# FFN tail: the up products are taken out of PSUM by VectorE with both factors, in place of a ScalarE copy and a GpSimd product

## The chip, the cores and the metric

The kernel runs on one core of a Trainium2 chip. The metric is the device time of one execution in microseconds (us). The core has five engines with a queue each: TensorE (matmuls and transposes, results into PSUM), VectorE, ScalarE, GpSimd and SyncE, which issues the DMAs. They wait for each other by semaphores only; VectorE also waits for its own earlier results by an explicit drain.

## The reference

Two layers over x of 8 batches, 128 tokens and 512 features: a cross attention with 32 heads, an FFN with quantized operands, a channel attention with a small convolution, and a routed low-rank FFN, each with a layernorm ahead and a residual sum behind. The change touches only the quantized FFN:

```python
def fake_quant(t, axis):
    s = jnp.max(jnp.abs(t), axis=axis, keepdims=True) / QMAX
    s = jnp.maximum(s, 1e-08)
    q = jnp.clip(jnp.round(t / s), -QMAX - 1.0, QMAX) * s
    return t + jax.lax.stop_gradient(q - t)

def qlinear(x, w):
    xq = fake_quant(x, axis=-1)
    wq = fake_quant(w, axis=1)
    return jnp.einsum('bsh,oh->bso', xq, wq)
gate = qlinear(x, w_gate)
up = qlinear(x, w_up)
h = jax.nn.silu(gate) * up
return qlinear(h, w_down)
```

The inner width (INTER) is 1376.

## The kernel before, in words

A token tile is one batch: 128 tokens on the partitions, 512 features. Attention runs over 64 steps (32 heads for four batches, then 32 heads for the other four). The FFN of the first four batches is done inside the second half of these steps. The FFN of the last four, k = 0 to 3, is done after the attention, in a tail of its own from about 942 us to 1013 us. The tail's order is written out by hand, once for each engine; every engine takes its own queue in order.

For a tile k of the tail:

- VectorE (`token_steps`) finds the tile's maximum and quantizes it (L1471 to L1480); TensorE transposes it (`token_transposes`), ScalarE brings the transposed tile to SBUF as bf16 integers (`tokens_out`, L953).
- TensorE multiplies it with the gate weights into the PSUM tensor pA of three banks, in three chunks of 512, 512 and 352 columns, four matmuls each (`gate_products`, L2043). VectorE takes each chunk out in one instruction that multiplies by the step of the row (y_steps) and by the step of the weight's column (w_row[0]): `gate_rows`, L1489. ScalarE makes silu of the whole gate (`gated_silu`, L969).
- TensorE then writes the up products into the same three banks (`up_products`, L2043 again). A chunk waits until VectorE has taken the gate's chunk out of that bank. ScalarE copies each chunk out with the row's step (`up_out`, L961), and GpSimd, which works on SBUF only, multiplies the copy by the column's step (`up_rows` in its block, L684). The gate products of the next tile wait for ScalarE's copies to have left the banks (semaphore up_copy).
- VectorE (`hidden`) multiplies silu and up (L1496, 1376 columns), takes the maximum (L1498), makes step and reciprocal (L1500, L1502) and quantizes into h_mag (L1506). TensorE transposes h_mag in eleven pieces (`hidden_transposes`), ScalarE brings them to SBUF (`hidden_out`, L976 and L977), TensorE makes eleven down products into pD (`down_products`, L2078), VectorE takes them out with both factors (`down_rows`, L1514).
- The sum with the residual is GpSimd's for tiles 0 and 1 (`add_down`, L690) and VectorE's for 2 and 3 (`z_stats`, L1523). The statistics of the next layer follow: `z_stats` and `z_shift` on VectorE, the reciprocal root on GpSimd (`z_rstd`, L695), the normalized tile on ScalarE for tiles 0 and 1 (`z_normal`, L983), a transpose, and the split into two branches, for tiles 0 and 1 on GpSimd (`branches`, L700 and L702).

On GpSimd z_rstd(0) stands behind the up products of tile 3, and add_down(0) ahead of them. There are two buffers each for silu and up, and one for gate and for h_mag. ra is the matrix of the router and the low-rank factors; TensorE sums it over the features (L2106), ScalarE and GpSimd centre it (L1025, L710).

Of the kernel before, what the change touches and what calls it, by code (L numbers as in the profile page):

```python
# [13 lines left out]
F32 = mybir.dt.float32  # L14
# [4 lines left out]
ALU = mybir.AluOpType  # L19
# [3 lines left out]
P = 128  # L23
# [29 lines left out]
def layers_kernel(nc, x, cT, mask, bias, ln_w, wq, wk, wv, wo, w_gate, w_up, w_down,  # L53
# [3 lines left out]
    def sbuf(name, shape, dt=F32, stack=ctx):  # L57
        return stack.enter_context(nc.sbuf_tensor(name, shape, dt))
# [4 lines left out]
    def sem(name):  # L63
        return ctx.enter_context(nc.semaphore(name))

    with ctx:
# [165 lines left out]
        silu = [sbuf(f"silu{i}", [P, INTER], F32, inner_ffn) for i in range(2)]  # L232
        up = [e_up, sbuf("up1", [P, INTER], F32, inner_ffn)]
        h_mag = sbuf("h_mag", [P, INTER], F32, inner_ffn)
# [70 lines left out]
        s_d_added = sem("d_added")  # L305
        s_h_prod = sem("h_prod")
        s_o_last = sem("o_last")
# [63 lines left out]
        s_up = sem("up")  # L371
        s_up_copy = sem("up_copy")
        s_v = sem("v")
# [177 lines left out]
        def _(pool):  # L551
# [127 lines left out]

            def up_rows(k):  # L680

                for j, (c0, c1) in enumerate(chunks):
                    pool.wait_ge(s_up_copy, CHUNKS * k + j + 1)
                    g.tensor_tensor(up[k % 2][:, c0:c1], up[k % 2][:, c0:c1], w_row[1][:, c0:c1],  # L684
                                    ALU.mult).then_inc(s_up, 1)

            def add_down(k):
# [19 lines left out]
            token_rstd(1, HB)  # L707
            up_rows(0)
            pool.wait_ge(s_ra_mean, 1)
            g.tensor_tensor(ra[:], ra[:], ra_mean[:].to_broadcast([P, KT, E + ER]), ALU.subtract).then_inc(s_ra, 1)  # L710
            up_rows(1)
            up_rows(2)
            add_down(0)
            up_rows(3)
            z_rstd(0)
# [20 lines left out]
        def _(act):  # L736
# [217 lines left out]

            def up_out(k):

                if k >= 2:
                    act.wait_ge(s_h_prod, k - 1)
                for j, (c0, c1) in enumerate(chunks):
                    act.wait_ge(s_u_proj, CHUNKS * (HB + k) + j + 1)  # L960
                    a.activation(up[k % 2][:, c0:c1], pA[:, c0:c1], ACT.Copy,  # L961
                                 scale=y_steps[:, HB + k:HB + k + 1]).then_inc(s_up_copy, 1)

            def gated_silu(k):
# [52 lines left out]
            for k in range(1, HB):  # L1017
                tokens_normal(k)
            up_out(0)
            tokens_out(1)  # L1020
# [4 lines left out]
            a.activation(ra_mean[:, 0, :], ra_bank, ACT.Copy, scale=1.0 / D).then_inc(s_ra_mean, 1)  # L1025
            up_out(1)
            gated_silu(1)
            hidden_out(0)
            up_out(2)
            gated_silu(2)  # L1030
            hidden_out(1)
            up_out(3)
            gated_silu(3)
# [66 lines left out]
        def _(dve):  # L1100
# [382 lines left out]
            def gate_rows(k, j):  # L1483
# [3 lines left out]
                if j == 0 and later(k):  # L1487
                    dve.wait_ge(s_silu, HB + k)
                v.scalar_tensor_tensor(out=gate[:, c0:c1], in0=pA[:, c0:c1], scalar=y_steps[:, HB + k:HB + k + 1],  # L1489
                                       in1=w_row[0][:, c0:c1], op0=ALU.mult, op1=ALU.mult).then_inc(s_gate, 1)  # L1490

            def hidden(k):

                dve.wait_ge(s_silu, HB + k + 1)
                dve.wait_ge(s_up, CHUNKS * (k + 1))
                v.tensor_tensor(silu[k % 2][:], silu[k % 2][:], up[k % 2][:], ALU.mult).then_inc(s_h_prod, 1)  # L1496
                dve.drain()
# [81 lines left out]
            dve.wait_ge(s_y_normal, HB - 1)  # L1579
            token_steps(2, HB)  # L1580
            for j in range(CHUNKS):
                gate_rows(1, j)
            hidden(0)
            for j in range(CHUNKS):
                gate_rows(2, j)
            hidden(1)
            for j in range(CHUNKS):
                gate_rows(3, j)
            down_rows(0)
            hidden(2)  # L1590
            z_stats(0)
# [133 lines left out]
        def _(pe):  # L1725
# [321 lines left out]
            def gate_products(k):  # L2047
                pe.wait_ge(s_y_qT, k + 1)
                for j in range(CHUNKS):
                    if later(k):  # L2050
                        pe.wait_ge(s_up_copy, CHUNKS * (k - 1) + j + 1)
                    tail_inner(k, j, 0).then_inc(s_g_proj, 1)

            def up_products(k):
                for j in range(CHUNKS):
                    pe.wait_ge(s_gate, CHUNKS * (HB + k) + j + 1)
                    tail_inner(k, j, 1).then_inc(s_u_proj, 1)
# [40 lines left out]
            up_products(0)  # L2098
            token_transposes(1)
            gate_products(1)  # L2100
            token_transposes(2)
            token_transposes(3)
            pe.wait_ge(s_e_split, HB + 1)
            pe.wait_ge(s_const_in, 16 * 6)
            for kt in range(KT):
                last = mm(ra_bank, ones[:], ra[:, kt, :], start=kt == 0, stop=kt == KT - 1)  # L2106
            last.then_inc(s_ra_sum, 1)
            up_products(1)
            gate_products(2)
            hidden_transposes(0)  # L2110
            up_products(2)
            down_products(0)
            gate_products(3)
            hidden_transposes(1)
            up_products(3)
            down_products(1)
            hidden_transposes(2)
            down_products(2)
# [150 lines left out]
```

## Time and profile before

| what | value |
|---|---|
| median of three runs | 1065.99 us (1065.75 to 1067.38) |
| the profiled execution | 1069.71 us |
| its span, first to last instruction | 1068.0 us |
| mean granted TensorE clock | 0.973 |
| busy share of the span | TensorE 93%, VectorE 65%, ScalarE 48%, GpSimd 44% |
| chain of waits: shares of the span | TensorE 79%, VectorE 7%, GpSimd 3%, ScalarE 2% |

The profile is of one execution. A busy share is an average over stages that have different limits, so the table says little about the tail, which is some 7% of the span. There the timeline of each engine, the chain of waits in order of time and the busy time by stretch are to be read. The granted clock is that of TensorE as a share of full speed: 0.50 is 1.2 GHz and 1.00 is 2.4 GHz.

### The profile page before, as it was taken

What the parts mean: (1) busy time and instruction counts of PE and PEld (TensorE: products, weight loads), DVE (VectorE), ACT (ScalarE), POOL (GpSimd) and SP (SyncE); (2) the same over time, 40 slices, a digit from 0 to 9 for tenths busy, and PEclk for the clock granted to TensorE, in tenths of its full rate; (3) what the DMA queues carried; (4) which work ended last, traced back from release to release, by engine and by line L of the source; (5) the groups of instructions that cost most, each with busy time, mean ns of one, the idle gap of its engine ahead of it and who ended that gap; (6) DMA issues with size and microseconds to landing.
All of it is one profiled execution on the core that took longest, in us unless ns stands there. A gap on an engine that the chain in (4) does not pass through costs nothing.

```text
span 1068.0 us, 18238 instructions
## 1 busy us (share of the span) xinstructions
PE 996.8 (93%) x6004; PEld 843.0 (79%) x6004; DVE 697.6 (65%) x1827; ACT 512.6 (48%) x1328; POOL 467.5 (44%) x366
## 2 busy tenths in 40 slices
PE   5999999999999999999999999999999999869376
PEld 4888888888888888888888888888888888734263
DVE  5567565666577767677564575566567557678755
ACT  4454444444444445445543544445355354345561
POOL 4555444444444555443354344346435334226241
PEclk9999999999999999999999999999999999969768
DMA  6422222223333332333322222213222221000002
GB/s 219 161 92 87 95 95 89 91 95 96 96 97 98 98 97 83 104 112 98 106 84 84 85 67 72 83 42 98 73 74 84 80 69 53 23 21 1 0 2 79
DMA packets 50412, 87.71 MB, mean 82 GB/s; under 512 B 6368, under 2 KB 15200, under 8 KB 50336
## 3 DMA queue, kind: packets, MB, share of 16 engines
q1 hardware_dynamic: 50336, 86.76, 25.4%
q8 instruction: 40, 0.66, 0.2%
q14 instruction: 36, 0.29, 0.1%
HBM read 84.64 MB, written 2.10 MB: 81 GB/s over the span
## 4 chain that ended last, share of the span: by engine, by line
PE 79%; DVE 7%; issue 6%; POOL 3%; DVEq 2%; ACT 2%; DMA 1%; SPq 0%; POOLq 0%; ACTq 0%
PE pX L1731 15%; PE pX L1733 14%; PE pX L1732 14%; PE pT L1983 5%; PE oacc L1731 5%; PE oacc L1732 5%; PE oacc L1733 5%; PE pS L1915 5%; PE pS L1736 2%; PE pA L2043 1%; POOL wv_lo L570 1%; PE pX L1848 1%; PE pX L1904 1%; PE pT L1904 1%; PE pX L1736 1%
## 5 line engine op out<-in xcount | busy, mean ns | idle before, releaser
L570 POOL TENSOR_TENSOR wq_lo<-raw_q,wq_hi 128x512 fp32r<-128x512 f32 x64 | 82.6, 1290 | 264.2 <-DVE prob L1376 257.9
L1731 PE MATMUL pX<-wv_lo,cT_hi 128*128 128x256 f32 x512 | 149.5, 292 | 0.2 <-ACT q_sb L740 0.2
L1359 DVE TENSOR_TENSOR score<-pS,b_mask 128x512 f32<-128x512 f32 x64 | 44.2, 691 | 156.8 <-PE pS L1915 144.7
L868 ACT ACTIVATE prob<-score,neg_max 128x128 f32<-128x128 f32 x256 | 99.8, 391 | 97.4 <-DVE neg_max L1362 97.4
L1732 PE MATMUL pX<-wv_hi,cT_lo 128*128 128x256 f32 x512 | 144.3, 282 | 0.0
L1733 PE MATMUL pX<-wv_hi,cT_hi 128*128 128x256 f32 x512 | 144.2, 282 | 0.0
L570 POOL TENSOR_TENSOR wv_lo<-raw_v,wv_hi 128x1024 fp32r<-128x1024 f32 x32 | 77.1, 2409 | 121.9 <-ACT wv_hi L740 121.9
L740 ACT ACTIVATE v_sb<-pX 128x512 f32<-128x512 f32 x64 | 38.2, 597 | 163.6 <-PE pX L1733 163.6
L1731 PE MATMUL pX<-xT_lo,wq_hi 128*128 128x512 f32 x252 | 104.4, 414 | 5.7 <-POOL wq_lo L570 5.0
L1731 PE MATMUL oacc<-wo_lo,aT_hi 128*128 128x512 f32 x256 | 101.8, 398 | 3.5 <-DVE aT_lo L1351 2.3
L1731 PE MATMUL pX<-cT_lo,wk_hi 128*128 128x512 f32 x252 | 103.0, 409 | 0.0
L1732 PE MATMUL oacc<-wo_hi,aT_lo 128*128 128x512 f32 x256 | 101.0, 395 | 0.0
L1733 PE MATMUL oacc<-wo_hi,aT_hi 128*128 128x512 f32 x256 | 100.8, 394 | 0.0
L1733 PE MATMUL pX<-cT_hi,wk_hi 128*128 128x512 f32 x252 | 99.3, 394 | 0.0
L1732 PE MATMUL pX<-xT_hi,wq_lo 128*128 128x512 f32 x252 | 98.8, 392 | 0.0
L1732 PE MATMUL pX<-cT_hi,wk_lo 128*128 128x512 f32 x252 | 98.7, 392 | 0.0
L1733 PE MATMUL pX<-xT_hi,wq_hi 128*128 128x512 f32 x252 | 98.6, 391 | 0.0
L1732 PEld LDWEIGHTS pX<-wv_hi,cT_lo 128*128 128x128 f32 x512 | 98.0, 191 | 0.0
L1731 PEld LDWEIGHTS pX<-wv_lo,cT_hi 128*128 128x128 f32 x512 | 97.0, 190 | 0.5 <-ACT q_sb L740 0.5
L1733 PEld LDWEIGHTS pX<-wv_hi,cT_hi 128*128 128x128 f32 x512 | 97.0, 189 | 0.0
L740 ACT ACTIVATE wk_hi<-raw_k 128x512 fp32r<-128x512 f32 x64 | 40.4, 632 | 113.7 <-PE pX L1733 104.5
L570 POOL TENSOR_TENSOR wk_lo<-raw_k,wk_hi 128x512 fp32r<-128x512 f32 x64 | 83.0, 1298 | 26.7 <-ACT wk_hi L740 21.4
(308 smaller groups left out, 2377.4 us busy)
## 6 DMA issues: line engine op xcount, KB each, us to landing
raw_k<-in_wk SPq DMA_DIRECT2D x64, 256.0 KB, 2.8
raw_q<-in_wq SPq DMA_DIRECT2D x64, 256.0 KB, 3.5
raw_v<-in_wv SPq DMA_DIRECT2D x32, 512.0 KB, 3.9
raw_o<-in_wo SPq DMA_DIRECT2D x64, 256.0 KB, 2.6
b_raw<-in_bias SPq DMA_DIRECT2D x64, 64.0 KB, 2.5
g_raw<-in_w_gate SPq DMA_DIRECT2D x16, 172.0 KB
g_raw<-in_w_up SPq DMA_DIRECT2D x16, 172.0 KB
f_raw<-in_w_down SPq DMA_DIRECT2D x4, 688.0 KB, 4.1
```

Of the source, the lines that this page charges most:

```text
L570: g.tensor_tensor(w_lo[c][:], w_raw[c][:], w_hi[c][:].bitcast(F32), ALU.subtract).then_inc(s_w_lo[c], 1)
L740: return a.activation(dst, src, ACT.Copy)
L868: e = a.activation(prob[:, b, :], score[:, b, :], ACT.Exp, bias=neg_max[:, b:b + 1], accum_out=row_sum[:, b:b + 1])
L1359: v.tensor_tensor(score[:], pS[:].rearrange("p (b s) -> p b s", b=HB), b_mask[:], ALU.add).then_inc(s_scored, 1)
L1731: mm(dst, lh, rl, start=start, stop=False, skip_group_check=lint)
L1732: mm(dst, ll, rh, start=False, stop=False, skip_group_check=lint)
L1733: return mm(dst, lh, rh, start=False, stop=stop, skip_group_check=lint)
L1736: return mm(dst, src, ident, is_transpose=True, start=True, stop=True)
L1848: last = mm(pX0[:], e_hqT[0:deep, k * S:(k + 1) * S], wdT[0:deep, k, :], start=k == 0, stop=k == IT - 1)
L1904: last = mm(bank[:, 0:c1 - c0], y_qT[:, kt * S:(kt + 1) * S], w_rowT[up_half][:, kt, c0:c1], start=kt == 0, stop=kt == KT - 1)
L1915: last = mm(pS[:, cols], q_sb[:, cols], k_sb[:, cols], start=True, stop=True)
L1983: last = mm(pT[:, cols], v_sb[parity][:, b, heads], pT_sb[:, cols], start=True, stop=True)
```

## The change

The up products are taken out of PSUM by VectorE with both factors in one instruction, in a new `up_rows(k, j)` of VectorE's block, which is called three times at the head of `hidden(k)`. ScalarE's `up_out` and GpSimd's `up_rows` are gone, and with them the semaphores h_prod and up_copy and the second buffer of up. The gate products of the next tile wait for VectorE's `up_rows`. The orders by hand are changed with it: on VectorE hidden(k) stands ahead of gate_rows(k+1), and gate_rows(3) behind hidden(2); on TensorE the token transposes of tiles 1 to 3 and the sum of ra stand together ahead of gate_products(1), and each turn of a tile is gate, hidden transposes of the tile before, up, down of the tile before. A drain stands ahead of the product of silu and up. The hunks that only remove semaphores are left out here.

```diff
--- before.py
+++ after.py
@@ -230,7 +230,7 @@
         t_y = sbuf("t_y", [P, HB, D], F32, inner_ffn)
         t_yqT = [sbuf(f"t_yqT{k}", [P, KT * S], BF16, inner_ffn) for k in range(HB)]
         silu = [sbuf(f"silu{i}", [P, INTER], F32, inner_ffn) for i in range(2)]
-        up = [e_up, sbuf("up1", [P, INTER], F32, inner_ffn)]
+        up = e_up
         h_mag = sbuf("h_mag", [P, INTER], F32, inner_ffn)
         inner_ffn.close()
         coef = sbuf("coef", [P, B, KT, S], F32, post)
@@ -677,13 +675,6 @@
                 g.tensor_tensor(t_yrs[:, first:last], t_yve[:, first:last], neg_half[:, 0:last - first],
                                 ALU.pow).then_inc(s_y_rstd, 1)
 
-            def up_rows(k):
-
-                for j, (c0, c1) in enumerate(chunks):
-                    pool.wait_ge(s_up_copy, CHUNKS * k + j + 1)
-                    g.tensor_tensor(up[k % 2][:, c0:c1], up[k % 2][:, c0:c1], w_row[1][:, c0:c1],
-                                    ALU.mult).then_inc(s_up, 1)
-
             def add_down(k):
 
                 pool.wait_ge(s_d_used, HB + k + 1)
@@ -705,13 +696,9 @@
             token_rstd(0, 1)
             pool.wait_ge(s_y_var, 2)
             token_rstd(1, HB)
-            up_rows(0)
             pool.wait_ge(s_ra_mean, 1)
             g.tensor_tensor(ra[:], ra[:], ra_mean[:].to_broadcast([P, KT, E + ER]), ALU.subtract).then_inc(s_ra, 1)
-            up_rows(1)
-            up_rows(2)
             add_down(0)
-            up_rows(3)
             z_rstd(0)
             add_down(1)
             branches(0)
@@ -952,15 +939,6 @@
                 act.wait_ge(s_y_trans, k + 1)
                 a.activation(t_yqT[k][:], y_bank[k].bitcast(I16), ACT.Copy, bias=-OFFSET).then_inc(s_y_qT, 1)
 
-            def up_out(k):
-
-                if k >= 2:
-                    act.wait_ge(s_h_prod, k - 1)
-                for j, (c0, c1) in enumerate(chunks):
-                    act.wait_ge(s_u_proj, CHUNKS * (HB + k) + j + 1)
-                    a.activation(up[k % 2][:, c0:c1], pA[:, c0:c1], ACT.Copy,
-                                 scale=y_steps[:, HB + k:HB + k + 1]).then_inc(s_up_copy, 1)
-
             def gated_silu(k):
 
                 act.wait_ge(s_gate, CHUNKS * (HB + k + 1))
@@ -1016,20 +994,16 @@
             act.wait_ge(s_y_shift, 1)
             for k in range(1, HB):
                 tokens_normal(k)
-            up_out(0)
             tokens_out(1)
             gated_silu(0)
             tokens_out(2)
             tokens_out(3)
             act.wait_ge(s_ra_sum, 1)
             a.activation(ra_mean[:, 0, :], ra_bank, ACT.Copy, scale=1.0 / D).then_inc(s_ra_mean, 1)
-            up_out(1)
             gated_silu(1)
             hidden_out(0)
-            up_out(2)
             gated_silu(2)
             hidden_out(1)
-            up_out(3)
             gated_silu(3)
             hidden_out(2)
             z_normal(0)
@@ -1489,11 +1463,20 @@
                 v.scalar_tensor_tensor(out=gate[:, c0:c1], in0=pA[:, c0:c1], scalar=y_steps[:, HB + k:HB + k + 1],
                                        in1=w_row[0][:, c0:c1], op0=ALU.mult, op1=ALU.mult).then_inc(s_gate, 1)
 
+            def up_rows(k, j):
+
+                c0, c1 = chunks[j]
+                dve.wait_ge(s_u_proj, CHUNKS * (HB + k) + j + 1)
+                v.scalar_tensor_tensor(out=up[:, c0:c1], in0=pA[:, c0:c1], scalar=y_steps[:, HB + k:HB + k + 1],
+                                       in1=w_row[1][:, c0:c1], op0=ALU.mult, op1=ALU.mult).then_inc(s_up, 1)
+
             def hidden(k):
 
+                for j in range(CHUNKS):
+                    up_rows(k, j)
                 dve.wait_ge(s_silu, HB + k + 1)
-                dve.wait_ge(s_up, CHUNKS * (k + 1))
-                v.tensor_tensor(silu[k % 2][:], silu[k % 2][:], up[k % 2][:], ALU.mult).then_inc(s_h_prod, 1)
+                dve.drain()
+                v.tensor_tensor(silu[k % 2][:], silu[k % 2][:], up[:], ALU.mult)
                 dve.drain()
                 v.tensor_reduce(h_s[:, 0:1], silu[k % 2][:], AX.X, ALU.max, apply_absolute_value=True)
                 dve.drain()
@@ -1578,16 +1561,16 @@
             gate_rows(0, 2)
             dve.wait_ge(s_y_normal, HB - 1)
             token_steps(2, HB)
+            hidden(0)
             for j in range(CHUNKS):
                 gate_rows(1, j)
-            hidden(0)
+            hidden(1)
             for j in range(CHUNKS):
                 gate_rows(2, j)
-            hidden(1)
+            down_rows(0)
+            hidden(2)
             for j in range(CHUNKS):
                 gate_rows(3, j)
-            down_rows(0)
-            hidden(2)
             z_stats(0)
             down_rows(1)
             z_shift(0)
@@ -2048,7 +2031,7 @@
                 pe.wait_ge(s_y_qT, k + 1)
                 for j in range(CHUNKS):
                     if later(k):
-                        pe.wait_ge(s_up_copy, CHUNKS * (k - 1) + j + 1)
+                        pe.wait_ge(s_up, CHUNKS * (k - 1) + j + 1)
                     tail_inner(k, j, 0).then_inc(s_g_proj, 1)
 
             def up_products(k):
@@ -2096,25 +2079,24 @@
             pe.wait_ge(s_x1_done, 2)
             gate_products(0)
             up_products(0)
-            token_transposes(1)
-            gate_products(1)
-            token_transposes(2)
-            token_transposes(3)
+            for k in range(1, HB):
+                token_transposes(k)
             pe.wait_ge(s_e_split, HB + 1)
             pe.wait_ge(s_const_in, 16 * 6)
             for kt in range(KT):
                 last = mm(ra_bank, ones[:], ra[:, kt, :], start=kt == 0, stop=kt == KT - 1)
             last.then_inc(s_ra_sum, 1)
+            gate_products(1)
+            hidden_transposes(0)
             up_products(1)
+            down_products(0)
             gate_products(2)
-            hidden_transposes(0)
+            hidden_transposes(1)
             up_products(2)
-            down_products(0)
+            down_products(1)
             gate_products(3)
-            hidden_transposes(1)
+            hidden_transposes(2)
             up_products(3)
-            down_products(1)
-            hidden_transposes(2)
             down_products(2)
             z_transposes(0)
             hidden_transposes(3)
```

## Rows read from the trace of the kernel before

**Rows 1.** Chain of waits, whole span, from the page: shares by engine.
```profile
PE 79%; DVE 7%; issue 6%; POOL 3%; DVEq 2%; ACT 2%; DMA 1%; SPq 0%; POOLq 0%; ACTq 0%
```

**Rows 2.** Chain of waits in order of time: start us, us, what.
```profile
979.99 2.55 POOL xr L690
982.53 4.04 POOL up L684 x3
...
999.74 3.42 PE pD L2078 x11
```

**Rows 3.** Busy us (instructions) by stretch: PE, PEld, DVE, ACT, POOL; clock, DMA share, GB/s.
```profile
953.80:957.20 3.40, 1.50 (x7) 0.52 (x7) 2.88 (x7) 2.50 (x4) 0.82 (x1) 0.99 0.40 132
957.20:960.60 3.40, 2.74 (x12) 1.26 (x9) 3.08 (x5) 1.73 (x4) 1.90 (x3) 0.52 0.00 0
...
966.00:984.00 18.00, 17.88 (x107) 9.24 (x105) 16.54 (x22) 12.00 (x18) 13.82 (x10) 1.00 0.00 1
984.00:994.00 10.00, 3.90 (x28) 2.18 (x29) 8.77 (x12) 2.81 (x4) 6.73 (x6) 1.00 0.00 0
...
1023.00:1032.00 9.00, 7.82 (x33) 6.56 (x33) 4.05 (x10) 6.03 (x16) 4.82 (x5) 0.50 0.00 1
```

**Rows 4.** VectorE's timeline: start us, us, instruction, count, [idle before and what ended it].
```profile
955.65 0.49 DVE L1480 TENSOR_SCALAR t_y<-t_y,t_yinv 128x512 f32<-128x512 f32 x1
...
959.16 2.60 DVE L1480 TENSOR_SCALAR t_y<-t_y,t_yinv 128x512 f32<-128x512 f32 x2
962.58 0.75 DVE L1489 SCALAR_TENSOR_TENSOR e_gate<-pA,y_steps,g_row 128x512 f32<-128x512 f32 x1 [0.81 <-PE pA L2043]
...
965.44 1.58 DVE L1496 TENSOR_TENSOR silu<-silu,e_up 128x1376 f32<-128x1376 f32 x1
...
969.25 0.95 DVE L1506 TENSOR_SCALAR h_mag<-silu,h_s 128x1376 f32<-128x1376 f32 x1
970.53 1.90 DVE L1489 SCALAR_TENSOR_TENSOR e_gate<-pA,y_steps,g_row 128x512 f32<-128x512 f32 x3 [0.34 <-ACT silu L969]
972.35 1.58 DVE L1496 TENSOR_TENSOR silu<-silu,up 128x1376 f32<-128x1376 f32 x1
...
977.14 2.11 DVE L1489 SCALAR_TENSOR_TENSOR e_gate<-pA,y_steps,g_row 128x512 f32<-128x512 f32 x3
...
985.60 0.75 DVE L1514 SCALAR_TENSOR_TENSOR e_down<-pD,h_steps,sd_row 128x512 f32<-128x512 f32 x1
987.11 1.22 DVE L1534 SCALAR_TENSOR_TENSOR t_zshift<-t_zmv,t_zrs 128x1 f32<-128x1 f32 x1 [0.76 <-POOL t_zrs L695]
988.25 1.58 DVE L1496 TENSOR_TENSOR silu<-silu,up 128x1376 f32<-128x1376 f32 x1
...
992.05 1.77 DVE L1506 TENSOR_SCALAR h_mag<-silu,h_s 128x1376 f32<-128x1376 f32 x1
```

**Rows 5.** TensorE's timeline, the same columns.
```profile
956.86 2.66 PE L2043 MATMUL pA<-wuT,t_yqT 128*128 128x512 bf16 x8 [1.63 <-DVE e_gate L1489]
...
960.65 4.20 PE L2043 MATMUL pA<-wgT,t_yqT 128*128 128x512 bf16 x12 [0.71 <-ACT t_yqT L953]
...
965.13 1.15 PE L2106 MATMUL pD<-ra,ones 128*128 128x136 f32 x8
...
971.37 2.49 PE L2043 MATMUL pA<-wuT,t_yqT 128*128 128x512 bf16 x12
...
999.53 3.61 PE L2078 MATMUL pD<-wdT,e_hqT 128*128 128x512 bf16 x11
```

**Rows 6.** Timelines of the weight loads, ScalarE and GpSimd, the same columns.
```profile
961.48 0.15 PEld L2043 LDWEIGHTS pA<-wgT,t_yqT 128*128 128x128 bf16 x1 [0.28 <-issue]
...
960.48 1.35 ACT L969 ACTIVATE silu<-e_gate 128x1376 f32<-128x1376 f32 x1
...
968.18 4.04 POOL L684 TENSOR_TENSOR up<-up,u_row 128x512 f32<-128x512 f32 x3
...
991.83 1.26 POOL L702 TENSOR_TENSOR split<-zT,split 128x512 f32<-128x512 f32 x1
```

## The prediction: how the up products on VectorE move the tail

> **What bounds the kernel now.** I read the shares of the chain of waits first: TensorE holds most of it [rows 1], but nearly all of that lies in the attention part before 949 us, which the change does not touch. So I read the chain again, from 949 us on, in order of time. The FFN tail has three pieces there. From 960.65 to about 979 us the chain lies on TensorE. Then it goes through GpSimd: the sum of token tile 0 (2.55 us) and the three up products of tile 3 (4.04 us) [rows 2]. From 988.25 us it is VectorE's chain: product, maximum and quantization of tile 3, whose last instruction, h_mag(3), starts at 992.05 and ends at 993.82 [rows 4]. Everything behind, the statistics of tiles 1 and 2, the transpose of z(1), the eleven down products of tile 3 (3.42 us on the chain [rows 2]) and the convolution, hangs on that end and keeps its code. So the question is when h_mag(3) ends after the change.
>
> The table by stretch says what the change runs into: from 966 to 984 us TensorE is busy 17.88 of 18.00 us and VectorE 16.54, while GpSimd has 13.82 [rows 3]. VectorE is 92% full in the stretch in which it is to take up more.
>
> **What goes.** GpSimd loses twelve products, three of them 4.04 us [rows 6], ScalarE twelve copies out of PSUM. ScalarE is never the last arrival in this stretch but for short pieces, so its copies are worth nothing by themselves. SP's queue issues nothing here.
>
> **What VectorE gets.** Twelve instructions with both factors, PSUM in, SBUF out. Their row exists already: the gate's three chunks have this very form, 1.90 us busy for three, and 1.82 us from the first to the next instruction (970.53 to 972.35) [rows 4]. Behind them stands a new drain; between dependent instructions here that costs 0.09 us. So 1.91 us for a tile, 7.64 us for four. A tile then costs VectorE 1.82 (gate) + 1.91 (up) + 4.7 (965.44 to the end of h_mag(0) at 970.20, less the overlap with the next) = 8.4 us, against 6.5 before. TensorE's share of a tile is two times 2.3 for gate and up (12 matmuls, 2.49 us in the row, which overlaps its neighbours [rows 5]), 2.3 for the eleven down products at the same 0.21 each, and 0.6 for eleven transposes of 128 columns, 7.5 us. VectorE becomes the bound.
>
> **What VectorE gets back**, place by place, up to the end of h_mag(3) [rows 4]:
> - The two quantizing instructions before tile 1 take 2.60 us together beside GpSimd's products; one alone takes 0.49, so two back to back, less the overlap of 0.04 to 0.08 that neighbours show, about 0.94. Gain 1.66: they end at 960.1 in place of 961.76, and up(0) is ready at 959.5, so hidden(0) starts at once.
> - The wait of 0.81 before gate(1), and the gate's three chunks of tile 1, which take 2.86 (962.58 to 965.44) since TensorE feeds them late; now gate(1) is produced long before it is wanted. Gain 0.82 + 1.04.
> - The wait of 0.34 for silu before gate(2), and 2.11 against 1.90 for gate(3). Gain 0.5.
> - Between down_rows(1) at 985.60 and the product of tile 3 at 988.25 lie 2.65 us, of which work is 0.78 (down_rows 0.75, of which some overlaps, and about 0.1 for the 128x1 instruction); the rest is z_rstd(0) queued in GpSimd behind the up products, and a 128x1 instruction of 1.22 us beside GpSimd's sum. Gain 1.87.
> - h_mag(3), 1.77 us beside GpSimd's branch products against 0.95 for h_mag(0). Gain 0.83.
>
> Together 6.8 us.
>
> **New waits.** Hand schedule by these durations, 0.1 us for a signal. hidden(0) 960.1; its product 962.0, when silu(0) (960.48 + 1.35 [rows 6]) is done; h_mag(0) ends 966.75. gate_rows(1) 966.7 to 968.5. On TensorE the hidden transposes now stand before up(1) and cannot start before 966.85; up(1) follows 967.5 to 969.85, so up_rows(1) ends 0.2 late. On ScalarE hidden_out(0) is queued behind silu(1), which waits for gate_rows(1): it starts at 969.9 in place of right behind its transposes, down(0) starts at 971.4, gate(2), which is moved behind down(0), ends at 976.3. VectorE wants its last chunk at 976.7, so this is covered with 0.4 us to spare. up(2) costs 0.3, up(3) nothing, as statistics and down_rows(1) lie before it. Stalls 0.5 us. Moving the transposes of tokens 2 and 3 and the router's sum (1.15 us [rows 5]) ahead of gate(1) costs nothing: gate(1) then ends at 964.0 to 966.0 and is first wanted at 966.7. Sum: 7.64 - 6.8 + 0.5 = **+1.3 us**; h_mag(3) ends at 995.1.
>
> **The clock of that gap.** TensorE's granted clock was 0.99 (2.4 GHz) from 953.80 to 957.20, with 1.50 of 3.40 us busy and a gap of 1.63 at its end, and it then fell: 0.52 (1.2 GHz) in the next stretch [rows 3, 5]. From 966 on it stayed at 1.00 with no such gap. The change makes one: where TensorE went from gate(1) straight on, it now has nothing between the end of gate(1), 964.0 if the clock has risen by then, and the transposes at 966.85, a gap of 2.8 us. If the clock falls there, up(1) runs at 1.2 GHz. A matmul of 512 columns then starts every 0.43 us (0.15 of weight load and 0.28 of issue [rows 6]) and not every 0.21; chunk 0 takes 1.7 and chunk 1 1.7 against 0.86 each, and up_rows(1) ends 1.7 us later. This is on VectorE's chain. Bounds 0 and 1.7; I take 1.7, since the gap is longer than the one after which the clock fell. Later gaps (1.5 us at most by the schedule) do not exceed it, and from 984 to 994 us the clock stayed at 1.00 with 3.90 of 10 us busy [rows 3].
>
> **Two more bounds.** The down products of tile 3 took 3.61 us with part of them at the low clock [rows 5]; at 2.4 GHz eleven are 2.5, all at 1.2 GHz 4.7. So -1.1 to +1.1; I take 0, since the idle time before them keeps its shape. And h_mag(3) may still meet the branch products of tile 0 (1.26 us [rows 6]), for those shift with it: 0 if it starts first, +1.1 if behind. The schedule has it waiting when the first of the pair ends, so 0.
>
> That VectorE and GpSimd hold each other up is in the rows: 2.60 us against 0.94 while a GpSimd product ran, and GpSimd's sum took 2.55 [rows 2] against 1.26 for another 128x512 instruction of it [rows 6]. The Trainium skill, "SBUF — State Buffer", section "SBUF: two separate sides", says why: a shared port pair is held for a whole instruction, and the other engine blocks. By that rule the new instructions, with one SBUF tensor each, hold nobody up, and the sum is as above; the trace agrees (the three gate chunks at 970.53 ran beside GpSimd's products of tile 1, 968.18 to 972.22, and were not stretched [rows 4, 6]). The Trainium skill, "Perfetto Trace Analysis", section "Optimizing Scalar/DVE Operations", speaks against the change: with a saturated VectorE, work is better on ScalarE or even GpSimd. It adds that between VectorE and GpSimd this might not help. By the first sentence the time goes up, by the second it stays; the trace so far bears out the first.
>
> **Total.** The profiled execution took 1069.71 us, its span 1068.0, 1.71 around it; the median of the runs is 3.72 lower, and I apply the difference to it. +1.3 + 1.7 = +3.0: 1065.99 + 3.0 = **1069.0 us** (a profiled span near 1071).
>
> **Rivals.**
> - The clock holds through the gap, or has not risen yet when gate(1) starts, so that gate(1) itself, at half speed, fills it. For: gate(1) ran mostly at the low clock before, its row of 4.20 us [rows 5]. Against: TensorE is now busy without a pause up to it. Then +1.3 alone: 1067.3, within 0.2%. 22%.
> - Faster. One mechanism: the clock's level in the routed stage and in the last down products. From 1023 to 1032 us the clock was 0.50 with 7.82 us of TensorE busy [rows 3]; the same work at 2.4 GHz would give back at most 3.9, with the down products 5.0. A shift of the whole stage may let the rise fall earlier in the work. It must give back over 3.4 us to make the kernel faster by 0.2%; fully, 1065.99 + 1.3 - 5.0 = 1062.3. Against: nothing in the change fills the idle time before that stage. 10%.
> - The costly ends come together: the gap's clock, all down products at 1.2 GHz, h_mag(3) behind the branch products: 3.0 + 1.1 + 1.1 = +5.2, 1071.2; with the low clock in a second tile, 1072.9. 18%.
>
> **Chances.** Forecast 50% (1068.2 to 1070.4 by itself), rivals 22, 10 and 18. 0.2% is 2.1 us, about what a measurement of this kernel tells from no change. Slower 0.50 + 0.18 = 0.68, same 0.22, faster 0.10. The range leaves out the faster case and the top of the costly one: 1066.2 to 1071.8.
>
> **What would show it.** Right: in the profile after, VectorE has next to no idle time from 960 to 995 us; twelve up instructions near 0.63 us; the quantizing pair under 1 us; hidden products 8.4 to 8.7 us apart; TensorE with gaps; h_mag(3) ending 995 to 997; a clock near 0.5 somewhere between 967 and 971. Wrong: VectorE waiting for TensorE in each tile (then the low clock rules and I am too low), or h_mag(3) ending before 994 (then an up instruction costs less than the gate's, or more waits went than I count).

## The result, and the profile after

| | before | after |
|---|---|---|
| median of the plain runs | 1066.49 us (1065.75 to 1067.38) | 1073.06 us (1072.49 to 1073.42) |
| ratio | | 1.0059, 95% interval 1.0043 to 1.0075 |
| profiled execution, span | 1069.71, 1068.0 | 1073.42, 1071.7 |

The change makes the kernel slower by 6.3 us by the ratio (the medians differ by 6.6); 3.0 were forecast, with a range up to 1071.8 us. Between the two profiled spans lie only 3.7 us. That is the first sign that the profile of before was not an ordinary one.

VectorE's timeline of the kernel after, as in [rows 4]: start us, us, instruction, count, idle before and what ended it. L1470 is the new up instruction, L1479 the product of silu and up, L1463 the gate's.

```profile
953.11 0.16 DVE L1555 SCALAR_TENSOR_TENSOR t_yshift<-t_ymv,t_yrs 128x3 f32<-128x3 f32 x1 [0.90 <-POOL t_yrs L675]
...
958.97 0.88 DVE L1454 TENSOR_SCALAR t_y<-t_y,t_yinv 128x512 f32<-128x512 f32 x2
959.77 1.90 DVE L1470 SCALAR_TENSOR_TENSOR e_up<-pA,y_steps,u_row 128x512 f32<-128x512 f32 x3
961.76 2.71 DVE L1479 TENSOR_TENSOR silu<-silu,e_up 128x1376 f32<-128x1376 f32 x1
...
966.67 0.94 DVE L1489 TENSOR_SCALAR h_mag<-silu,h_s 128x1376 f32<-128x1376 f32 x1
967.52 1.89 DVE L1463 SCALAR_TENSOR_TENSOR e_gate<-pA,y_steps,g_row 128x512 f32<-128x512 f32 x3
970.77 0.75 DVE L1470 SCALAR_TENSOR_TENSOR e_up<-pA,y_steps,u_row 128x512 f32<-128x512 f32 x1 [1.35 <-PE pA L2026]
972.47 0.75 DVE L1470 SCALAR_TENSOR_TENSOR e_up<-pA,y_steps,u_row 128x512 f32<-128x512 f32 x1 [0.95 <-PE pA L2026]
973.65 0.58 DVE L1470 SCALAR_TENSOR_TENSOR e_up<-pA,y_steps,u_row 128x352 f32<-128x352 f32 x1 [0.42 <-PE pA L2026]
974.32 1.59 DVE L1479 TENSOR_TENSOR silu<-silu,e_up 128x1376 f32<-128x1376 f32 x1
...
983.42 1.59 DVE L1479 TENSOR_TENSOR silu<-silu,e_up 128x1376 f32<-128x1376 f32 x1
...
993.77 1.59 DVE L1479 TENSOR_TENSOR silu<-silu,e_up 128x1376 f32<-128x1376 f32 x1
...
997.57 0.94 DVE L1489 TENSOR_SCALAR h_mag<-silu,h_s 128x1376 f32<-128x1376 f32 x1
```

GpSimd's and TensorE's timelines of the same kernel, beside [rows 5]:

```profile
961.69 1.33 POOL L700 TENSOR_TENSOR ra<-ra,ra_mean 128x544 f32<-128x544 f32 x1 [8.61 <-ACT ra_mean L1002]
```
```profile
961.13 2.49 PE L2026 MATMUL pA<-wgT,t_yqT 128*128 128x512 bf16 x11
967.67 1.35 PE L1719 MATMUL pTb<-ident_b,h_mag 128*128 128x128 bf16 x11 [4.05 <-DVE h_mag L1489]
968.81 4.79 PE L2026 MATMUL pA<-wuT,t_yqT 128*128 128x512 bf16 x12
...
1004.21 4.33 PE L2061 MATMUL pD<-wdT,e_hqT 128*128 128x512 bf16 x11
```

And its busy time by stretch, the columns of [rows 3]:

```profile
962.00:966.00 4.00, 1.56 (x8) 0.68 (x7) 3.93 (x2) 0.00 (x0) 1.02 (x1) 1.00 0.00 0
966.00:974.00 8.00, 6.33 (x26) 3.23 (x27) 5.04 (x10) 2.63 (x3) 0.00 (x0) 0.57 0.01 2
974.00:984.00 10.00, 7.89 (x46) 3.87 (x46) 9.52 (x14) 2.64 (x3) 1.27 (x1) 1.00 0.00 0
```

From 974 to 984 us VectorE is busy 95% of the time and TensorE 79%; in [rows 3] it was 92 and 99%. The other two things to see are a first product that takes 2.71 us while its three sisters take 1.59, beside GpSimd's centring of ra (it starts 0.07 us ahead of the product), and the granted clock of 0.57 between 966 and 974 us, where VectorE waits three times for up(1), 2.7 us in all.

To compare executions that start the tail a little earlier or later, I count from one instruction that all have and that the change does not touch, the shift of the tokens (t_yshift; 953.11 us above). Each number is a time in VectorE's timeline less that (starts of the products of silu and up of tiles 0 and 2 and of down_rows(3), the end of h_mag(3)), and the span's end less that. The short names are those of the experiments; each line is one execution.

| execution | product 0 | product 2 | end of h_mag(3) | down_rows(3) | end of the span |
|---|---|---|---|---|---|
| before, on record | 12.13 | 26.51 | 40.51 | 49.86 | 114.69 |
| before_again | 10.66 | 25.02 | 39.03 | 49.02 | 111.94 |
| before_third | 9.76 | 23.79 | 37.79 | 47.05 | 111.70 |
| after | 8.65 | 30.31 | 45.40 | 55.47 | 118.59 |
| after_again | 8.65 | 28.11 | 44.30 | 54.95 | 118.81 |
| ra_late | 8.94 | 28.39 | 43.47 | 52.88 | 117.69 |
| fill16 | 8.65 | 27.62 | 42.71 | 52.81 | 115.91 |
| both12 | 8.84 | 26.70 | 41.79 | 52.08 | 115.36 |
| twice | 10.45 | 31.69 | 48.59 | 57.77 | 122.52 |
| zshift | 9.76 | 23.79 | 37.55 | 46.95 | 111.77 |
| gates_first | 9.59 | 23.63 | 37.63 | 46.95 | 111.69 |
| best1 | 10.18 | 24.92 | 38.68 | 48.60 | 111.51 |
| zshift2 | 9.76 | 23.80 | 35.49 | 46.06 | 109.04 |
| best2 | 9.59 | 23.61 | 35.31 | 45.99 | 109.09 |

### The profile page after: what moved, and what is told of

It is laid out like the page before. It is cut to its first block, busy times and chain, and to the rows that moved or that the text cites. A ratio compares the mean times of both kernels' runs of the same rounds, so it can differ in the third digit from the quotient of the medians.

```text
span 1071.7 us, 18208 instructions
## 1 busy us (share of the span) xinstructions
PE 995.3 (93%) x5988; PEld 841.7 (79%) x6004; DVE 702.3 (66%) x1839; ACT 505.6 (47%) x1316; POOL 451.1 (42%) x354
## 4 chain that ended last, share of the span: by engine, by line
PE 77%; DVE 9%; issue 6%; POOL 3%; ACT 2%; DVEq 2%; DMA 1%; SPq 0%; POOLq 0%; ACTq 0%
PE pX L1714 15%; PE pX L1716 14%; PE pX L1715 14%; PE pT L1966 5%; PE oacc L1714 5%; PE oacc L1715 5%; PE oacc L1716 5%; PE pS L1898 5%; PE pS L1719 2%; POOL wv_lo L568 1%; PE pT L1887 1%; PE pX L1831 1%; PE pX L1887 1%; PE pX L1719 1%; DMA raw_k<-in_wk 1%
```

## The experiments

### More profiles of the two kernels

No edit. The kernel before is profiled twice more, and the kernel after once more.

> The kernel before, unchanged, for a second profile. The profiled execution on record took 1069.71 us where its plain runs have a median of 1066.5; the changed kernel's took 1073.42 against 1073.1. Theory P (that one execution was late by where TensorE's clock rose and fell in the stages behind the FFN tail): the second profile has a span near 1065 and its tail ends h_mag(3) again near 993.8, with the difference behind 1003 us. Rival Q (a profile adds 3 us to this kernel): span near 1068 again.

> The kernel before once more. Counted from the shift of the tokens, the product of tile 2 started at 26.51 us in the profile on record, at 25.02 in before_again and at 23.79 in zshift, whose code is the same up to there. Theory B (the kernel before is bound by TensorE from up(0) to up(2), so its start moves with the clock that these products get, 4.20 or 2.50 us for gate(1)): this look lies between 23.7 and 26.6, and goes with the duration of up(0) and gate(1). Rival: the profile on record is the usual one, and this shows 26.5 again.

> The changed kernel once more. By theory B it is bound by VectorE and does not profit from an early high clock: its first product starts 8.6 to 9.0 us after the shift, takes 2.7 beside the centring of ra, and the end of h_mag(3) lies at 43 to 45.5, by how much of up(1) runs at the low clock. If the start varies as in the kernel before, by 2.7 us, theory B is wrong.

Measured: before_again 1067.48 us, span 1065.7; before_third 1067.49, span 1065.7; after_again 1074.45, span 1072.7. VectorE and TensorE in before_again, then the same in before_third:

```profile
962.60 1.90 DVE L1489 SCALAR_TENSOR_TENSOR e_gate<-pA,y_steps,g_row 128x512 f32<-128x512 f32 x3 [1.07 <-ACT silu L969]
...
991.02 1.77 DVE L1506 TENSOR_SCALAR h_mag<-silu,h_s 128x1376 f32<-128x1376 f32 x1
```
```profile
961.31 2.50 PE L2043 MATMUL pA<-wgT,t_yqT 128*128 128x512 bf16 x12 [0.71 <-ACT t_yqT L953]
```
```profile
990.02 1.77 DVE L1506 TENSOR_SCALAR h_mag<-silu,h_s 128x1376 f32<-128x1376 f32 x1
```
```profile
957.55 1.64 PE L2043 MATMUL pA<-wuT,t_yqT 128*128 128x512 bf16 x8 [1.37 <-DVE e_gate L1489]
...
960.31 2.50 PE L2043 MATMUL pA<-wgT,t_yqT 128*128 128x512 bf16 x12 [0.91 <-ACT t_yqT L953]
```

The same kernel ends h_mag(3) at 40.5, 39.0 or 37.8 us. The clock of up(0) and gate(1) goes with it: up(0)'s last eight matmuls took 2.66 us on record [rows 5], 2.86 in before_again and 1.64 in before_third, and gate(1) 4.20, 2.50 and 2.50. The execution on record was the slowest of the three, and its idle 0.81 us and stretched gate chunks of tile 1 [rows 4] were that clock. In before_again the three chunks take 1.90 us, behind a wait of 1.07 us for silu; in before_third VectorE does not wait for them at all. The quantizing pair ahead of them took 2.60, 1.90 and 2.17 us.

Theory B had the range right. That TensorE bounds this stretch is true of two executions of the three. In before_third the chain of waits leaves TensorE behind the router's sum and reaches the product of tile 1 over GpSimd:

```profile
964.64 1.90 POOL ra L710
966.53 4.00 POOL up L684 x3
970.63 1.59 DVE silu L1496
```

Rival Q is out, since the spans are 1065.7 us. Part of Theory P fell: it had h_mag(3) end where it did, and the difference behind. About half of the difference of the spans to before_again, 1.5 us of 2.75 counted from the shift, lies ahead of h_mag(3).

The start of the kernel after does not take part in this: its first product starts at 8.65 us in both profiles, though up(0) had the high clock in the first (1.63 us) and mostly the low one in the second (2.70 us). Two things differ behind it. VectorE, then GpSimd in after_again:

```profile
962.54 1.59 DVE L1479 TENSOR_TENSOR silu<-silu,e_up 128x1376 f32<-128x1376 f32 x1
...
996.15 2.04 DVE L1489 TENSOR_SCALAR h_mag<-silu,h_s 128x1376 f32<-128x1376 f32 x1
```
```profile
963.66 1.66 POOL L700 TENSOR_TENSOR ra<-ra,ra_mean 128x544 f32<-128x544 f32 x1 [9.81 <-ACT ra_mean L1002]
...
996.20 1.26 POOL L693 TENSOR_TENSOR split<-zT,split 128x512 f32<-128x512 f32 x1
```

My expectation for the product missed: 2.71 us in one execution and 1.59 in the other. The router's sum stands behind up(0), so with the low clock the centring comes later, here 1.12 us after the product has started, and the product is not stretched. And h_mag(3) takes 2.04 us beside a branch product of tile 0, in place of 0.94: 1.1 us of the 44.30 are that.

### Holding back the centring of ra

```diff
             pool.wait_ge(s_ra_mean, 1)
+            pool.wait_ge(s_gate, CHUNKS * (HB + 2) + 1)
             g.tensor_tensor(ra[:], ...
```

> The changed kernel, with GpSimd's centring of ra held back until VectorE has taken the first gate chunk of tile 2. Theory L (the first product of silu and up took 2.71 us in place of 1.58 since it met that centring on the shared port): it takes 1.6, h_mag(0) ends 1.1 us earlier and the time falls by 1.1, to about 1072.0. Rival C (only TensorE's clock in the gap before up(1) matters, VectorE waits there anyway): the product is shorter, the wait for up(1) longer by as much, and the time stays at 1073.

Measured: 1072.41 us, ratio to before 1.0052 (1.0035 to 1.0069), 0.7 us under the kernel after and not to be told from it by the intervals. The rows say more:

```profile
962.35 1.59 DVE L1480 TENSOR_TENSOR silu<-silu,e_up 128x1376 f32<-128x1376 f32 x1 [0.39 <-ACT silu L948]
...
970.11 0.75 DVE L1471 SCALAR_TENSOR_TENSOR e_up<-pA,y_steps,u_row 128x512 f32<-128x512 f32 x1 [1.22 <-PE pA L2027]
971.36 1.24 DVE L1471 SCALAR_TENSOR_TENSOR e_up<-pA,y_steps,u_row 128x512 f32<-128x512 f32 x2 [0.50 <-PE pA L2027]
```

The product takes 1.59 us with the centring out of its way (it ran at 978.23), as Theory L had it, but this run does not show the cause. In this profile up(0) had the low clock (2.99 us), and in after_again, with the low clock and no edit, the product takes 1.59 us as well. What speaks for Theory L is the set of the profiles: 2.71 us in both executions in which the centring starts just ahead of the product (after, and fill16 below, 961.27 against 961.34), 1.59 in every other one of the changed kernel. No run holds the centring back in an execution in which the two would have met. Rival C is not borne out: the waits for up(1) are 1.7 us, not longer than the 2.7 of the kernel after, and they are 1.7 in after_again too (0.78 and 0.96).

### Filling TensorE's gap

```diff
             gate_products(1)
+            for i in range(16):
+                mm(pZ[:], ident_b[:], w_rowT[0][:, i % KT, 0:512], start=True, stop=True)
             hidden_transposes(0)
```

> The changed kernel with 16 matmuls of 128x512 into an unused bank between gate_products(1) and hidden_transposes(0), 3.45 us of work at 2.4 GHz in a gap of 4.05 us; their result is used by nothing. Theory C (the gap lets the clock fall, and up(1) at 1.2 GHz makes VectorE wait 2.7 us): granted clock 1.00 from 962 to 990 us, the waits of 1.35, 0.95 and 0.42 us before the up chunks of tile 1 fall to under 0.3 in all, time 2.9 us less, about 1070.2. Rival W (VectorE waits for up(1) because the transposes stand ahead of it, whatever the clock): waits of over 1 us stay, time within 1 us of 1073.

Measured: 1071.34 us, ratio 1.0046 (1.0030 to 1.0063). VectorE, then the busy time by stretch:

```profile
968.98 2.10 DVE L1470 SCALAR_TENSOR_TENSOR e_up<-pA,y_steps,u_row 128x512 f32<-128x512 f32 x3
```
```profile
966.00:974.00 8.00, 6.08 (x37) 2.92 (x36) 7.63 (x10) 2.64 (x3) 0.00 (x0) 1.00 0.00 0
```

The clock stays at 1.00, up(1)'s three chunks take 2.10 us with their waits in place of 3.46 and 1.35 ahead of them, and h_mag(3) ends at 42.71 in place of 45.40, 2.7 earlier where 2.9 were expected. Theory C holds, and W falls: 0.2 us of waits are left. This pair, after and fill16, has the high clock at up(0) and the stretched first product in both. The other pair, ra_late and both12 below, has the low clock at up(0) and no stretched first product; there the filled gap is worth 43.47 - 41.79 = 1.7 us. The gap ahead of the hidden transposes was 4.05 us in the first case and 2.90 in the second. The plain runs of after and fill16 differ by 1.7 us, the lower of the two; how often each kind of execution comes, no run tells.

### Both together

The two edits above, with 12 matmuls.

> Both of these together, with 12 matmuls in place of 16 since the gap is 1.1 us shorter. If the two costs are separate and additive: 1073.1 - 1.1 - 2.9 = 1069.1, h_mag(3) ends at about 994.5 us, which would leave the 1.3 us of the sum for VectorE's added work alone against 993.6. If one hides behind the other: no faster than the better of the two.

Measured: 1071.46 us, ratio 1.0037 (1.0022 to 1.0051). h_mag(3) ends at 41.79 us: 3.6 before the kernel after, where the two expected effects add to 4.0. 41.79 is to the digit what the prediction's sum has without a clock term (995.1 less 953.31). So VectorE's side of the sum was right as a whole, and still the kernel is 0.37% slower than before, 3.9 us and not the 1.3 of the sum. What was wrong is the other side of the comparison: 40.51 as the kernel before's end. Against the other two profiles 41.79 is +2.8 and +4.0.

The expected 1069.1 us missed for a reason of the same kind. It takes two effects, read in one execution of the kernel after in which both were full, off the median of the plain runs; in after_again one of the two was not there and the gap was 2.62 us. By the plain runs it is the other expectation that came: 1071.46 is no faster than fill16's 1071.34.

### The up instructions twice

```diff
                 dve.wait_ge(s_u_proj, CHUNKS * (HB + k) + j + 1)
+                v.scalar_tensor_tensor(out=up_more[:, c0:c1], in0=pA[:, c0:c1], ...)
                 v.scalar_tensor_tensor(out=up[:, c0:c1], in0=pA[:, c0:c1], ...
```

> The kernel of both12 with each of VectorE's twelve up instructions issued twice, the first time into a buffer that nothing reads. Theory V (VectorE is the bound of the tail, so its added work stands on the path in full): 4 x 1.8 = 7.3 us more on VectorE, less the 0.5 us of waits that it covers; the end of h_mag(3), counted from the shift of the tokens (t_yshift), goes from 41.8 to 48.6 us and the time rises by 6.8, to about 1078. Rival T (TensorE or the chain over the transposes is the bound, and the up instructions lie half beside it): under 4 us more.

Measured: 1077.97 us, ratio 1.0102 (1.0087 to 1.0118), 6.5 us over both12. VectorE at tile 3, from the shift at 953.98:

```profile
994.04 0.74 DVE L1472 SCALAR_TENSOR_TENSOR up_more<-pA,y_steps,u_row 128x512 f32<-128x512 f32 x1
994.70 0.74 DVE L1474 SCALAR_TENSOR_TENSOR e_up<-pA,y_steps,u_row 128x512 f32<-128x512 f32 x1
...
1001.63 0.94 DVE L1493 TENSOR_SCALAR h_mag<-silu,h_s 128x1376 f32<-128x1376 f32 x1
```

h_mag(3) ends at 48.59, 6.80 later, as Theory V had it. Work on VectorE stands on the path in full in the changed tail, but for the waits that it covers; Rival T, with under 4 us, is out.

### Taking GpSimd out of VectorE's way in the kernel before

If GpSimd's chain cost the kernel before 1.9 us at tile 3, moving one small step should bring them back without more work for VectorE. The edits are to the kernel before; in zshift the step stands ahead of the drain, in zshift2 (the second diff) behind the maximum.

```diff
                 v.tensor_tensor(silu[k % 2][:], ...).then_inc(s_h_prod, 1)
+                if k == HB - 1:
+                    z_shift(0)
                 dve.drain()
...
             down_rows(1)
-            z_shift(0)
             hidden(3)
```

> The kernel before with one small step moved: z_shift(0) stands between the product and the maximum of tile 3, not ahead of the product, so VectorE does not wait there for GpSimd's up products and root. Theory G (GpSimd's chain cost the kernel before 1.9 us at this place, as the prediction's sum has it): the product of tile 3 starts 1.6 us earlier (it still waits for the last up product), h_mag(3) ends 37.4 us after the shift of the tokens in place of 39.0, time 1.6 us less, 1065.3. Rival H (the place is covered, what hangs on z_shift(0) is then late): within 0.5 us of the kernel before.

Measured: ratio 1.0000 (0.9991 to 1.0009). VectorE and GpSimd:

```profile
983.69 1.59 DVE L1496 TENSOR_TENSOR silu<-silu,up 128x1376 f32<-128x1376 f32 x1 [0.33 <-POOL up L684]
985.20 1.23 DVE L1536 SCALAR_TENSOR_TENSOR t_zshift<-t_zmv,t_zrs 128x1 f32<-128x1 f32 x1
...
988.65 1.93 DVE L1508 TENSOR_SCALAR h_mag<-silu,h_s 128x1376 f32<-128x1376 f32 x1
```
```profile
984.06 2.35 POOL L690 TENSOR_TENSOR xr<-xr,e_down 128x512 f32<-128x512 f32 x1
```

From product 2 to product 3 it is now 6.87 us in place of 8.44: the 1.57 are there. From product 3 to the end of h_mag(3) it is 6.89 in place of 5.57: GpSimd's sum takes 2.35 us in place of 1.26, beside the product; z_shift(0), a 128x1 instruction, takes 1.23 beside the sum, and h_mag(3) 1.93 beside the branch products. Neither theory had this: the gain is real, and 1.3 us of it are given back before h_mag(3) ends, where VectorE and GpSimd meet again.

```diff
                 v.tensor_reduce(h_s[:, 0:1], silu[k % 2][:], ...)
+                if k == HB - 1:
+                    z_shift(0)
```

> The kernel before with z_shift(0) behind the maximum of tile 3. In the run zshift, with it ahead of the maximum, the product of tile 3 came 1.57 us earlier, but 1.3 us were given back: z_shift(0) took 1.23 us beside GpSimd's sum and h_mag(3) 1.93 beside the branch products. Theory S (all of it is the shared port, so a step later both are clear of it): z_shift(0) takes 0.15, h_mag(3) 0.95 and ends before the branch products begin; from the product of tile 2 to the end of h_mag(3) 11.8 us in place of 14.0, time 2.2 less, about 1064.7. Rival D (what follows h_mag(3) does not wait for it, or GpSimd's steps collide elsewhere): within 0.7 us of the kernel before.

Measured: 1065.05 us against 1066.55, ratio 0.9986 (0.9976 to 0.9995).

```profile
983.91 1.59 DVE L1496 TENSOR_TENSOR silu<-silu,up 128x1376 f32<-128x1376 f32 x1 [0.33 <-POOL up L684]
985.60 1.59 DVE L1498 TENSOR_REDUCE h_s<-silu 128x1 f32<-128x1376 f32 x1
987.10 0.15 DVE L1536 SCALAR_TENSOR_TENSOR t_zshift<-t_zmv,t_zrs 128x1 f32<-128x1 f32 x1
987.81 0.94 DVE L1508 TENSOR_SCALAR h_mag<-silu,h_s 128x1376 f32<-128x1376 f32 x1
```

z_shift(0) is 0.15, h_mag(3) 0.94, and from product 2 to the end of h_mag(3) it is 11.7 us (14.0 before), as Theory S expected; of 2.3 us in the tail the plain runs show 1.5. GpSimd's sum had ended at 986.63, so z_shift(0) at the end of the maximum no longer met it.

### Gate chunks of tile 0 first

```diff
-            gate_rows(0, 0)
+            for j in range(CHUNKS):
+                gate_rows(0, j)
             dve.wait_ge(s_y_normal, 1)
             token_steps(1, 2)
-            gate_rows(0, 1)
-            gate_rows(0, 2)
```

> The kernel before with VectorE taking out all three gate chunks of tile 0 before it quantizes tile 1. Up(0) on TensorE then follows gate(0) without its gap of 1.6 us. Theory E (from 957 to 984 us the kernel before is bound by TensorE, so an earlier start counts): gate(1) starts 1.2 us earlier and h_mag(3) with it, time 1.2 less, 1065.7. Rival: quantizing tile 1 becomes late by the 1.2 us of the two chunks, gate(1) starts when it did, and the time stays.

> The kernel before with both of these. If both count and add: 1.6 + 1.2 = 2.8 us less than the kernel before, 1064.1. If the first start is not on the path, the 1.6 alone.

> The same with all gate chunks of tile 0 taken out before tile 1 is quantized, which alone measured nothing (ratio 1.0001). If that stays so: the time of zshift2. If the earlier start shows once GpSimd is out of the way: up to 1.2 us less, 1063.5.

Measured: alone 1.0001 (0.9992 to 1.0010), no gain, so Theory E is not borne out. Counted from the shift, gate(1) starts at 5.76 us, 0.55 earlier than in before_third and not 1.2, and product 0 at 9.59 against 9.76. As in before_third the chain then goes over GpSimd's centring (2.29 us here) and its three up products (4.01), which took 1.90 and 4.00 there. With zshift (best1) 1066.50 us, ratio 0.9994 (0.9985 to 1.0003), in place of the expected 1064.1; as in zshift, z_shift(0) takes 1.23 us and h_mag(3) 1.93. With zshift2 (best2) 1064.63 us, ratio 0.9979 (0.9970 to 0.9988): faster than both kernels, but from zshift2 alone it can't be told, the intervals overlap.

## Why the prediction was wrong

**VectorE's added work: right.** Twelve instructions, 1.89 to 1.90 us for three where nothing is waited for, on the path in full (twice), and the sum for the tail hits both12's h_mag(3) to 0.1 us. The forecast of the mechanism, VectorE as the bound, holds. That the hit is so close is in part luck: the sign "hidden products 8.4 to 8.7 us apart" came for tiles 0 and 1 only (8.72 us in both12, then 9.14 and 10.35), because down_rows and z_stats stand between the later ones.

**What VectorE gets back: the step that failed.** The gains of 0.82 + 1.04 at gate(1), and a part of the 1.66 at the quantizing pair, were read off one execution in which TensorE's clock was low at up(0) and gate(1). In before_again VectorE's wait and stretch at gate(1) are 1.07 us, in before_third none, and the pair takes 1.90 and 2.17 us in place of 2.60. So the first product of the kernel before starts 1.5 or 2.4 us earlier than on record, and h_mag(3) ends 1.5 or 2.7 us earlier, while the kernel after, bound by VectorE, starts its first product at 8.65 us in both profiles. The prediction saw that the profiled execution was 3.72 us over the median, and then carried a difference made against it over to the median. Of the five profiles whose code is the same up to product 2 (the three of before, zshift and zshift2), three start it at 23.8 us, as before_third does; the 26.51 on record is the latest. The gain at z_shift(0) (0.16, no wait) came as stated. That of h_mag(3) came in the first profile of the kernel after (0.94) and not in the second (2.04).

**The clock of the gap: right in place; in size right in one kind of execution.** Taken at 1.7 us with a gap of 2.8. With the low clock at up(0) the gap was 2.62 and 2.90 us and cost 1.7 (ra_late against both12). With the high clock there the first product was stretched, the gap was 4.05 us and cost 2.7 (after against fill16), since the transposes (1.35 us against 0.78) and the third chunk ran at the low clock as well.

**Not seen: the centring of ra.** It moved with the router's sum. In the kernel before on record it starts at 966.67 us, 1.23 after the product of tile 0, and runs mostly beside the maximum; in the first profile after it starts 0.07 ahead of the product. The prediction costed TensorE's part of that move at nothing, and left out the GpSimd instruction that follows from it. It goes with 1.12 us in the first profile (2.71 less 1.59) and with 0 in after_again. The cause is read from the rows and not shown by an edit.

**The last down products and the rivals.** The down products of tile 3 were taken at 3.61 us, with bounds of 2.5 and 4.7. They took 4.33 and 4.90 us in the kernel after, the second above the bound, and 4.25 and 3.50 in the two later profiles of the kernel before, so this term moves in both. Neither rival in which the time stays or falls came. The costly one comes nearest in size: in after_again all three of its terms are there (a low clock in up(1), 4.90 us for the down products, h_mag(3) beside a branch product), in the first profile the first of them and a part of the second.

**What the 6.3 us are made of.** The forecast had h_mag(3) of the kernel after at 43.5 us from the shift (40.51 + 3.0). ra_late has 43.47; the kernel itself has 45.40 and 44.30, so 1.9 or 0.8 more, by the stretched first product with its longer gap, or by the late h_mag(3). The kernel before ends it 1.5 or 2.7 us earlier than the forecast took. The forecast's 3.0 and these two make between 5.3 and 7.6 us, by which pair of profiles is taken; the plain runs have 6.3. What lies behind down_rows(3) varies by 2 us among executions of one kernel (64.8, 62.9 and 64.7 us from there to the end in the three profiles of before), so how the 6.3 us split between tail and routed stage stays open. So does the share of the new orders on VectorE and TensorE and of the new drain, which no run takes apart.

## What to carry to other kernels

A row is of one execution. Where an engine that has a variable clock sets the pace, take a second profile before a wait there is booked as a gain of the change, above all when the profiled execution lies off the median. That holds for the experiments too: an edited and an unedited execution can differ by the clock and not by the edit, and a cost seen in one execution can't be taken off a median. When a step is moved, follow what it triggers to the engines behind it: here that is a GpSimd instruction two hops on, which goes with up to 1.1 us. Two instructions that stretch each other need not be removed; the small one can be put behind a reduction, by whose end the other is over, which got back 1.5 us here with no work moved to another engine.

## What the runs showed of the hardware

TensorE's granted clock did not follow the length of the last gap alone. After a gap of 1.63 us ahead of up(0)'s second part it fell in the profile of before [rows 3, 5] and in after_again (up(0) taking 2.70 us); after one of 1.64 us at the same place in the first profile of the kernel after it stayed high, up(0) taking 1.63 us:

```profile
956.66 1.63 PE L2026 MATMUL pA<-wuT,t_yqT 128*128 128x512 bf16 x8 [1.64 <-DVE e_gate L1463]
```

After gaps of 4.05, 2.90 and 2.62 us ahead of the hidden transposes of tile 0 (after, ra_late, after_again) up(1) ran partly at the low clock each time (4.79, 3.76 and 4.18 us in place of 2.5), and with 0.60 and 0.20 us left of the gap (fill16, both12) it did not.
A 128x1 instruction on VectorE took 1.23 us in place of 0.15 beside a GpSimd sum, and a maximum of 128x1376, with one tensor read, was 1.58 to 1.59 us in every execution, also beside GpSimd's centring and its products. The Trainium skill, "SBUF — State Buffer", section "Who interferes with whom", has both: two SBUF inputs contend with a GpSimd instruction that reads SBUF, a reduction never does. The rows agree.
